# Graph attention on one core: groups of up to 16 nodes that begin at every 484th edge, in blocks of 4 x 128 edges, and a planning stage that searches rows of 256 edges

## What is computed

```python
def _L0_gnn_ref(x, W, a_src, a_dst, edge_W, edge_b, bias, edge_attr, edge_index):
    n = x.shape[0]
    h = (x @ W.T).reshape(n, H, D)          # 8 heads of 32
    src, dst = (edge_index[0], edge_index[1])
    h_src = h[src]
    h_dst = h[dst]
    alpha = jnp.einsum('ehd,hd->eh', h_src, a_src) + jnp.einsum('ehd,hd->eh', h_dst, a_dst)
    enc = jax.nn.relu(edge_attr @ edge_W.T + edge_b).reshape(-1, H, D)
    alpha = alpha + jnp.sum(enc * h_dst, axis=-1)
    alpha = jnp.where(alpha >= 0, alpha, 0.2 * alpha)
    amax = jax.ops.segment_max(alpha, dst, num_segments=n)
    ex = jnp.exp(alpha - amax[dst])
    denom = jax.ops.segment_sum(ex, dst, num_segments=n)
    attn = ex / jnp.maximum(denom[dst], 1e-10)
    out = jax.ops.segment_sum(h_src * attn[..., None], dst, num_segments=n)
    return out.reshape(n, H * D) + bias
...
x = x + _L0_gnn_ref(_layernorm(x), ..., edge_attr_3, edge_index)
x = x + _L0_ffn_ref(_layernorm(x)[None], ...)[0]     # 8 experts, the best 2 of each node
x = x + _L1_gnn_ref(_layernorm(x), ..., edge_index)  # the same attention without enc
x = x + _L1_ffn_ref(_layernorm(x)[None], ...)[0]     # 8 experts, the best 1
```

## Time and profile before

| what | value |
|---|---|
| median of 3 runs | 8268.06 us |
| lowest and highest | 8252.19, 8271.06 us |
| the profiled execution: its own time, its span | 8254.24 us, 8252.5 us |
| planning stage | 0 to 336.3 us |
| first edge stage | 528.8 to 3371 us |
| second edge stage | 4859.0 to 7441 us |
| blocks of both edge stages (L984 in the page) | 784, that is 392 each |
| busy over the span: PE, DVE, ACT, POOL | 75%, 56%, 35%, 52% |

### The profile page before, as it was taken

How to read it: one execution, slowest core, us unless ns; L and a number is a source line. 1 busy time by engine, 2 the same in 40 slices (tenths; PEclk the granted TensorE clock), 3 DMA queues, 4 the chain that set the end, 5 groups by cost and what they waited for, 6 DMA issues and landing times. The chain is left out here.

```text
span 8252.5 us, 163611 instructions
## 1 busy us (share of the span) xinstructions
PE 6179.6 (75%) x32278; PEld 4927.6 (60%) x32278; DVE 4611.0 (56%) x15207; ACT 2868.2 (35%) x5703; POOL 4286.7 (52%) x4324
## 2 busy tenths in 40 slices
PE   0279999999999999319999176666666666663793
PEld 0166666666666666319998165555555555552792
DVE  2337777777777777611111447777777777764005
ACT  0025555555555555102222023333333333331120
POOL 0027777777777777140000437777777777771103
PEclk9989999999999999659999589999999999995896
DMA  1446666666666666625555436666666666674453
GB/s 48 144 106 155 153 153 153 153 154 155 153 153 153 153 153 154 188 87 174 186 180 184 135 91 160 159 160 160 158 157 161 159 160 159 159 147 140 162 187 129
DMA packets 1526846, 1244.98 MB, mean 151 GB/s; under 512 B 1112600, under 2 KB 1256875, under 8 KB 1500779
## 3 DMA queue, kind: packets, MB, share of 16 engines
q1 hardware_dynamic: 1316073, 648.43, 31.0%
q0 software_dynamic: 205472, 580.68, 25.4%
q10 hardware_dynamic: 5256, 15.41, 0.6%
HBM read 1106.73 MB, written 137.14 MB: 151 GB/s over the span
## 5 line engine op out<-in xcount | busy, mean ns | idle before, releaser
L732 POOL DMA_INDIRECT e_rows<-sc_table,e_idx x3900 | 3878.0, 994 | 1409.0 <-issue 1084.7
L791 PE MATMUL e_ps_o<-e_rows,e_pt 128*128 128x256 f32 x7840 | 1892.1, 389 | 475.1 <-ACT e_pt L848 455.9
L791 PEld LDWEIGHTS e_ps_o<-e_rows,e_pt 128*128 128x128 f32 x7840 | 1454.5, 194 | 735.4 <-issue 562.7
L776 PE MATMUL e_ps_s<-e_ident,e_arep 128*128 128x128 f32 x7840 | 1048.1, 282 | 344.9 <-ACT e_arep L842 341.7
L776 PEld LDWEIGHTS e_ps_s<-e_ident,e_arep 128*128 128x128 f32 x7840 | 962.1, 195 | 465.8 <-issue 460.5
L836 ACT ACTIVATE e_encr<-e_ps_e 128x640 f32<-128x640 f32 x786 | 553.5, 704 | 1353.4 <-PE e_ps_e L763 1340.0
L984 DVE CUSTOM_DVE_ANT_0 e_x<-e_ps_s,e_mask 128x640 f32<-128x640 f32 x784 | 645.1, 823 | 641.4 <-PE e_ps_s L776 631.5
L772 PE MATMUL e_ps_s<-e_encr,e_bd 128*128 128x512 f32 (+1 forms) x3136 | 956.0, 448 | 0.8 <-ACT e_encr L836 0.8
L842 ACT COPY e_arep<-e_rows 128x640 f32<-128x640 f32 x786 | 570.7, 726 | 993.9 <-DMA e_rows<-sc_table,e_idx 993.5
L1514 POOL DMA_INDIRECT c_g<-sc_yb,f_slot_i x147 | 170.9, 1162 | 1346.5 <-PEq L1496 1288.3
L772 PEld LDWEIGHTS e_ps_s<-e_encr,e_bd 128*128 128x128 f32 x3136 | 504.0, 191 | 481.9 <-issue 481.9
(11 more groups left out here) (271 smaller groups left out, 6126.7 us busy)
## 6 DMA issues: line engine op xcount, KB each, us to landing
e_dstb<-sc_dstp SPq DMA_DIRECT2D x792, 320.0 KB
x_w<-in_L_ffn_W_dram SPq DMA_DIRECT2D x112, 1024.0 KB
e_rows<-sc_table,e_idx POOLq DMA_INDIRECT x3960
x_w<-in_L_ffn_w_dram SPq DMA_DIRECT2D x60, 1024.0 KB
sc_xb<-r_zero SPq DMA_DIRECT2D x24, 1024.0 KB
x_xin<-sc_xb SPq DMA_DIRECT2D x86, 256.0 KB
sc_yb<-x_y SPq DMA_DIRECT2D x82, 256.0 KB
e_at<-sc_attrp SPq DMA_DIRECT2D x396, 45.0 KB
```

Source lines behind the costliest of these rows:

```text
L732: pool.indirect_dma_start(rows[0:CK, k, j, :], None, dr["table"][:, :], bass.IndirectOffsetOnAxis(idx[0:CK, k, j:j + 1], 0)).then_inc(s_ro ...
L776: mm = nc.tensor.matmul(banked(ps_s)[:, j, :], arep[0:CK, p, j, :, :].rearrange("p t h -> p (t h)"), ident[0:CK, 0:CK], start=not first, s ...
L791: mm = nc.tensor.matmul(ps_o[:, p, 0:D], pt[0:CK, p, j * P:(j + 1) * P], rows[0:CK, k, j, 0:D], start=(j == 0), stop=(j == CH - 1))
```

## The change

- **Groups in place of windows.** A group still has up to 16 nodes, but may begin at any node. The list is cut at every 484th edge (`STEP`), which gives `NI` = 427 intervals; the node that holds edge 484 i begins a group, and if an interval has more than 16 nodes, further groups follow after every 16. A block is 4 chunks, 512 edges (`CH` = 4). `blk` holds the group's first node in place of a window number. A result of a group with fewer than 16 nodes is written over 16 rows, and the next group's store overwrites the rows that aren't its own.
- **Planning.** Every 484th element is fetched by strided transfers of single words (`vg`), groups are numbered by a running sum over the intervals, and for each of 896 group numbers (`WT` = 7) the first node and the end are found by 21 sums over 512 elements. The search goes over 806 rows of 256 edges: 14 counts over 806 elements, 14 gathers of 256 elements with four buffers, 14 counts over 256.
- **The attributes' split** moves to ACT (three copies) and POOL (two subtractions); `attrp` has 12 rows, read three times by one transfer in `load`.
- **Loads in planning** are issued in the order destinations, attributes, sources; VectorE waits for the destinations alone.
- PSUM tiles of the edge stages hold one bank (512 columns) per buffer, with an index by p for `ps_s` and `ps_t` and by half for `ps_e`. What is waited for stays the same.

```diff
-NW = -(-N // WIN)
-WT = -(-(NW + 1) // P)
-MEAN = -(-E * WIN // N)
-CH = -(-(MEAN + 2 * int(MEAN ** 0.5)) // P)
+STEP = 484
+NI = -(-E // STEP)
+IT = -(-NI // P)
+MAXW = NI + -(-N // WIN)
+WT = -(-(MAXW + 1) // P)
+RB = 256
+NR = P * EC // RB
+
+CH = 4
...
         @block.gpsimd
+            nc.gpsimd.tensor_tensor(rest[:, :, :], attr[:, :, :].rearrange("p e c -> p c e"), part[:, 0, :, :],
+                                    ALU.subtract).then_inc(s_rest, 1)
...
             for s in range(2):
+                pool.wait_ge(s_rix, s + 1)
                 for t in range(WT):
                     k = s * WT + t
-                    if k:
-                        pool.wait_ge(s_cp, k)
-                    pool.indirect_dma_start(rows[:, 0, :], None, (dr["pmax"] if s == 0 else dr["smin"])[:, :],
-                                            bass.IndirectOffsetOnAxis(rix[:, s, t:t + 1], 0)).then_inc(s_wg, 16)
-                    pool.wait_ge(s_wg, 16 * (k + 1))
+                    if k >= 4:
+                        pool.wait_ge(s_cp, k - 3)
+                    pool.indirect_dma_start(found[:, k % 4, :], None,
+                                            (dr["pmax"] if s == 0 else dr["smin"]).rearrange("(r k) -> r k", k=RB),
+                                            bass.IndirectOffsetOnAxis(rix[:, s, t:t + 1], 0)).then_inc(s_wg[k % 4], 16)
...
+                for s in range(2):
+                    sp.dma_start(vg[:, s, 0:full], dr["pmax"][s * STEP:s * STEP + full * P * STEP:STEP].rearrange("(t p) -> p t", p=P)).then_inc(s_grid, 16)
...
+            for t in range(WT):
+                for n, upto, of in ((0, 2, 0), (1, 2, 1), (2, 3, 0)):
+                    done(nc.vector.scalar_tensor_tensor(junk[:, 0:IT * P], irow[:, upto, :], jcol[:, t:t + 1], irow[:, of, :],
+                                                        ALU.is_le, ALU.mult, accum_out=wv[:, n, t:t + 1]))
...
             def load(b, k, r):
-                w = sp.value_load(tab[0:1, r, 0:1], min_val=0, max_val=NW)
+                n = sp.value_load(tab[0:1, r, 0:1], min_val=0, max_val=N)
...
-                    sp.dma_start(at[:, k, :], dr["attrp"][:, bass.ds(e, BE)]).then_inc(s_load[k], 16)
-                    sp.dma_start(htw[:, k, :, :], dr["hT"].rearrange("(c p) n -> p c n", p=P)[:, :, bass.ds(w * WIN, WIN)]).then_inc(s_load[k], 16)
+                    sp.dma_start(at[:, k, :], dr["attrp"][:, bass.ds(e, BE)].unsqueeze(0).to_broadcast([3, PARTS, BE])).then_inc(s_load[k], 16)
+                    sp.dma_start(htw[:, k, :, :], dr["hT"].rearrange("(c p) n -> p c n", p=P)[:, :, bass.ds(n, WIN)]).then_inc(s_load[k], 16)
...
-                nc.tensor.matmul(banked(ps_e)[:, 0:4, :], lhs, cols[:, 0:4, :], start=True, stop=True)
-                nc.tensor.matmul(banked(ps_e)[:, 4, :], lhs, cols[:, 4, :], start=True, stop=True).then_inc(s_enc, 1)
+                nc.tensor.matmul(ps_e[:, half, :], lhs, at[:, k, :], start=True, stop=True).then_inc(s_enc, 1)
```

More of the change, by code:

```diff
@@ L93, in plan_phase @@
         rix = sb("rix", [P, 2, WT], I32)
[L94 to L95 removed]
+        found = sb("found", [P, 4, RB], F32)
+        junk = sb("junk", [P, 1024], F32)
         lohi = sb("lohi", [P, 2, WT], F32)
@@ L100, in plan_phase @@
         off = sb("off", [P, WT], F32)
-        win = sb("win", [P, WT, 2], F32)
+        win = sb("win", [P, WT, 3], F32)
         cumrow = sb("cumrow", [P, WT * P], F32)
@@ L165, in _ @@
             sp.dma_start(attr[P - 1:P, 0:E_LAST, :], v[(P - 1) * EC:E, :].rearrange("(p e) c -> p e c", p=1)).then_inc(s_attr, 16)
-            sp.wait_ge(s_in, 64)
-            sp.wait_ge(s_pad, 6)
+            v = io["src"]
+            sp.dma_start(src_i[0:P - 1, :], v[0:(P - 1) * EC].rearrange("(p e) -> p e", p=P - 1)).then_inc(s_bl, 16)
+            sp.dma_start(src_i[P - 1:P, 0:E_LAST], v[(P - 1) * EC:E].rearrange("(p e) -> p e", p=1)).then_inc(s_bl, 16)
+            sp.wait_ge(s_final, 1)
+            sp.dma_start(dr["pmax"].rearrange("(p e) -> p e", p=P), pmax[:, :]).then_inc(s_out, 16)
+            sp.dma_start(dr["smin"].rearrange("(p e) -> p e", p=P), smin[:, :]).then_inc(s_out, 16)
+            sp.wait_ge(s_out, 32)
+            sp.wait_ge(s_zp, 2)
+            with nc.allow_non_contiguous_dma(reason="every STEP-th and every RB-th word of a sorted list, once"):
+                for s in range(2):
+                    sp.dma_start(vg[:, s, 0:full], dr["pmax"][s * STEP:s * STEP + full * P * STEP:STEP].rearrange("(t p) -> p t", p=P)).then_inc(s_grid, 16)
+                    left = dr["pmax"][(full * P + s) * STEP:E:STEP]
+                    sp.dma_start(vg[0:left.shape[0], s, full:full + 1], left.rearrange("(p e) -> p e", e=1)).then_inc(s_grid, 16)
+                for s, name in ((0, "pmax"), (1, "smin")):
+                    sp.dma_start(brow[0:1, s, :], dr[name][RB - 1:P * EC:RB].rearrange("(a r) -> a r", a=1)).then_inc(s_grid, 16)
+            sp.wait_ge(s_in, 32)
+            sp.wait_ge(s_bl, 32)
             for tile, name, r in ((dst_i, "dstp", 0), (src_i, "srcp", 1)):
@@ new lines, in _ @@
+            ts(vg[:, :, :], vg[:, :, :], float(N), None, ALU.min)
+            done(nc.vector.memset(vg[0:1, 0, 0:1], 0.0))
+            tt(iv[:, 0, :], vg[:, 1, :], vg[:, 0, :], ALU.subtract)
+            whole(iv[:, 1, :], iv[:, 0, :], 1.0 / WIN, 0.5 - 0.5 / WIN)
+            v.sem_inc(s_iv, 1)
+            v.wait_ge(s_pe, 4)
+            done(nc.vector.memset(offi[:, 0:1], 0.0))
+            for t in range(1, IT):
+                tt(offi[:, t:t + 1], offi[:, t - 1:t], pt[:, 7 + t:8 + t], ALU.add)
@@ L835, in relu @@
                     hold(act, s_s, b - 1, s_pa)
-                nc.scalar.activation(chunks(encr[:, p, half, :]), banked(ps_e), ACT.Relu).then_inc(s_relu, 1)
+                nc.scalar.activation(encr[:, p, half, :], ps_e[:, half, :], ACT.Relu).then_inc(s_relu, 1)
             def repeat(b, k, turns, p):
@@ L1565, in scratch @@
     dr = {}
-    for name, shape, dt in (("pmax", [P, EC], F32), ("smin", [P, EC], F32), ("win", [WT * P, 2], F32), ("nblk", [1, 4], I32),
-                            ("dstp", [EP], I32), ("srcp", [EP], I32), ("attrp", [K_ENC, EP], BF16),
+    for name, shape, dt in (("pmax", [P * EC], F32), ("smin", [P * EC], F32), ("win", [WT * P, 3], F32), ("nblk", [1, 4], I32),
+                            ("dstp", [EP], I32), ("srcp", [EP], I32), ("attrp", [PARTS, EP], BF16),
                             ("blk", [MAXB, 2], I32), ("blkf", [MAXB, 1], F32),
```

235 lines of the change are left out of this document (131 added, 104 removed).

## The result

The changed kernel takes 8346.69 us in the median of 3 runs (8345.6 to 8352.28), against 8268.06 before: 1.0102 times as long, 95% interval 1.0079 to 1.0125. It is slower, where 8090 us and faster were forecast. The profiled execution has a span of 8343.9 us.

The account below looks back on a forecast made before the run. PE was taken to bound the first edge stage and POOL the second, with SP's queue last in the first afterwards. 8254 + 78 - 209 - 36 = 8087 us, predicted as 8090, range 7880 to 8220.

Parts of the forecast that it names:

- What bounds each stage: Before: PE sets the first edge stage, POOL the second; after: SP's queue the first, neck and neck with POOL in the second.
- First edge stage: SP's queue becomes last at an unchanged 38.9 us a round, 73 rounds; PE needs 34.0 us a round: +78 us.
- The upper bound of the step: First edge stage: a round costs the queue's mean without its waits for VectorE, 39.6 us; stage 129 us longer.
- Rival 2: Loading attributes with 12 rows repeated three times issues slower on SP's queue; at +0.5 us per block 8306 us; 13%.
- Rival 1: PE stays the first edge stage's bound because the queue's gaps shrink; round 34.0 us, total 7685 us; 13%.
- Second edge stage: POOL and SP's queue nearly equal, 31.5 us a round for 38.6: -209 us.
- Planning: Loads, counts and gathers before the edge stages end at about 300 us for 336.3: -36 us, bounds 0 and -60.

## Why the prediction was wrong

1. *What bounds each stage*: right. The queue had the slack that was read (one further transfer is nearly free, a second costs 2.8% more), and after the change the queue is last in both stages, in the second together with POOL: one transfer less per block gains 3%, one more in the second stage alone costs 3%.
2. *First edge stage, the step that failed* (its term of the sum, +78 us): "SP's queue has the same instructions as before, one for one; only the transfers are smaller. So its 38.9 us a round stands." It took the transfer of `at` for one of the others, at 0.36 us. It measures 0.84, and the block is 0.59 us dearer with what follows it. Of the 262 us between the forecast's +78 and the measured +340, undoing this one edit brings back 259. The upper bound of the step, 39.6 us a round, came from rows that had no such transfer, and so did not hold the price. That 36 plain rows give 39.03 us and 8084, so near to 38.9 and 8090, is in part luck: the fetch costs 2.4 us a round and not 2.09, against which a block takes 6.10 us and not 6.13 (its step from `htw` to the store, read as 1.64 at the least, is 1.59 in the median); and in the total planning gained 12 us less than forecast, the second stage 21 more.
3. *Rival 2* was this mechanism, with the right place; its price at +0.5 us, 8306 us, is 41 below the time measured, which is the 0.59 us a block in place of 0.5 (40 us). Its sign, an issue of `at` over 0.5 us, is what the trace shows. It got 13% because "the shapes of the loop's other transfers differ widely without their issue differing". They differ in size and in partitions, and `htw` has three dimensions too, but rows that are read in two steps (twelve, then again from the first) were in none of them, so they were no evidence. The listing of instructions did differ: it has 36x1x512 for this transfer, where before it has 36x640. The x1 alone was no sign, since `idx` has one as well (128x4x1) and issues in 0.39 us. From 0.38 us more the forecast saw no gain; it was 0.50 from `at` to `htw` and 0.59 in all.
4. Of the rule in the Trainium skill, "DMA: Bandwidth & Descriptors", section on why a DMA increments its semaphore by 16, on the engines that divide the slowest dimension, the runs show no effect on the time here: with 12 for 3 the kernel was slower by 20 us, not faster. How many engines either transfer used wasn't read.
5. *Rival 1* (PE stays the bound) is out: in the changed kernel the slices of a block add up to 0.40 + 0.45 + 0.33 + 0.33 + 0.84 + 0.40 + 0.36 = 3.11 of 6.65 us, and yet the longer issue costs its full length. The rule of the Trainium skill, "Perfetto Trace Analysis", section "What DMA-bound means", by which a bound sequencer shows a track solid with slices, would have missed it.
6. *Second edge stage*: the round of 31.44 us is the forecast 31.5. The stage gained 229 for 209 us; 73 x 31.44 - 65 x 38.56 = -211 are the rounds, and 18 lie before and behind the loop, a part that wasn't read further. The same part is 12 us in the first stage (73 x 42.64 - 65 x 42.48 = +352 for +340). The forecast had left it out.
7. *Planning*: -19.6 for -36. The first gather was due at 208 us and came at 217:

```profile
177.00 0.17 DVE L285 TENSOR_SCALAR pl_vg<-pl_vg 128x8 f32<-128x8 f32 x1 [125.84 <-DMA pl_brow<-sc_smin]
...
190.50 0.75 DVE L342 SCALAR_TENSOR_TENSOR pl_junk<-pl_irow,pl_jcol 128x512 f32<-128x512 f32 x1
...
216.98 1.09 POOL L165 DMA_INDIRECT pl_found<-sc_pmax,pl_rix  x1 [57.62 <-DVE pl_rix L353]
...
241.48 0.17 DVE L363 SCALAR_TENSOR_TENSOR pl_lohi<-pl_cnt,pl_lohi 128x14 f32<-128x14 f32 x1
251.84 0.40 SPq L208 DMA_DIRECT2D sc_win<-pl_win  x1
```

The strided words have landed at 177 (172 forecast), the numbering takes 13.5 us (10), the 21 sums 16.7 (17) and the counts were priced right. The gathers take until 241.5: with four buffers the fifth waits 2.9 us for a count. The store of `win` is at 251.8 (237), and from there to the end it is 64.8 us (63). All four steps that miss are small, and all in one direction. The 12 stores of `attrp` for 36 brought nothing here: with 36 again, planning ends at 312.2 us for 316.7. In the kernel before they cost time because they ran beside the table's turns (DMA engines busy all of 258 to 300 us); in both new versions they are done by then. So the transfer that repeats the rows cost 259 us and saved none.

## What to carry to other kernels

If a queue with one instruction stream is near its limit, every edit to it must be priced one by one, also where the listing has the same instructions before and after: a transfer whose rows are read in two steps is not the one that reads them plainly. If the price stands in no row, it deserves the range and not the mean, above all where it multiplies by the number of blocks. And before a cut of a fifth per block, ask what stays per block: the queue's work did, so its cure was fewer transfers (one less per block was worth 3%), and not smaller ones.

## What the runs showed of the hardware that was not expected

- On SP's queue a transfer into 36 partitions that reads 3 x 12 rows of 512 has an issue of 0.82 to 0.85 us, with or without repetition, and in the order 12 x 3 one of 0.91; 36 plain rows with the same data have 0.36. The issue of `htw` behind it is 0.40 us for 0.38, and the step from there to the store 1.68 for 1.59.
- The queue waits 1.1 us in the mean for its fetch of 12 table entries in the kernel before, and 2.3 us with two more small transfers per block; with one more it is 1.7.
- At the slower pace the kernel before took 10221 to 10472 us, and the changed one 3.4% less than it, not 1.0% more. It isn't a property of a chip: two of the three chips on which it was seen ran at the usual pace at another time. In the trace of the changed kernel planning ends at the usual 316.6 us, and the two edge stages take 3722 and 3302 us (3185.5 and 2356.1). The queue's transfers often start 0.7 to 0.8 us apart, or twice that, at whatever length their issue has elsewhere:

```profile
1503.05 0.02 SPq L744 DMA_DIRECT2D e_idx<-sc_srcp  x1
1503.80 0.01 SPq L745 DMA_DIRECT2D e_dstb<-sc_dstp  x1
1504.54 0.69 SPq L746 DMA_DIRECT2D e_wc<-sc_wcol  x1
1505.99 0.01 SPq L747 DMA_DIRECT2D e_nf<-sc_blkf  x1
1507.41 0.11 SPq L749 DMA_DIRECT2D e_at<-sc_attrp  x1
1507.72 0.40 SPq L750 DMA_DIRECT2D e_htw<-sc_hT  x1
```

  (timeline of the variant with 3 x 12 rows and no repetition). Something holds the transfers back there, and a long issue is mostly hidden: 36 plain rows gain 0.4%. What it is stays open, and so does why the change pays there: the kernel before has no trace at that pace. A difference of 1% on a kernel bound by a queue of small transfers holds for a given pace of those transfers.
